# A four-layer transformer block on one core: the order of linear attention, its handover to the expert layer, and the place of three operations in later loops

## Chip, cores and metric

One core of one Trainium2 chip. The metric is device microseconds of one launch, the median of three runs.

## What is computed

The input x is 16 sequences of 256 tokens of 128 features, float32. Four layers follow, each in the same frame:

```
x = x + layernorm(layer(layernorm(x)))
layer 1 (LA):  qkv = u @ W_qkv.T; 16 heads of 8; q = (elu(q)+1)*8**-0.5, k = elu(k)+1
               num, den = causal sums of (q k) v and of q k;  (num / max(den, 1e-6)) @ W_out.T
layer 2 (MOE): s = softmax(u @ centroids.T + biases), the 2 largest of 16 experts weigh Wr[e] u + br[e]
               u + routed + (sum of Ws[e] u + bs[e]) / 2
layer 3 (SA):  layernorm with gain and bias, 16 heads of 64, rotary positions, softmax attention, @ w_out
layer 4 (FFN): gated 128 -> 512 with ternary weights, two 512 -> 512 with gelu, 512 -> 128
```

## The kernel before

Everything stays in SBUF: X holds all 16 sequences (two tiles of 128 tokens each), XnT the normalised transpose that the next layer reads. Each layer is a software pipeline over the 16 sequences: each engine has its own program, a step function called for i = 0 to 15 (the first two or four and the last two written out, the middle in a hardware loop, two steps per turn), and semaphores tie the programs together. The order on each engine is written by hand. An engine runs its instructions in order, so a wait holds back all that stands behind it.

PE (TensorE) does matmuls and transposes, DVE (VectorE) most elementwise work and statistics, ACT (ScalarE) exponentials and copies from PSUM, POOL (GpSimd) the roots of the norms (`rstd_pool`, L363 and L365), the update of X (`residual_pool`, L370), the copy of a sequence's columns into xT (L402), some masks and products.

**Norm.** A norm piece on DVE is statistics (L298), their aggregate (L303), and an application (L314 for the layer's output y, L343 for X), with POOL's root between. Norm 1 has one output norm and one input norm (pieces 0 to 3), norm 2 (after the experts) one output and two input norms (nine fine pieces). PE transposes xn (L383), ACT copies it to XnT (L392).

**Linear attention** (24 to 206.8 us). In step i, PE does scores(i) for two halves (L498), the out product of i-2 (L604), sums(i-1, 1) (L552 for the state, L560), the norm's transposes of i-3 (L383), the v product of i+1 (L454), the turn back (L572), the turn of o (L592), sums(i, 0), the q and k product of i+2 (L443), the state product (L536). DVE: state (L543), divide (L577 to L582), xn (L343), masks (L507), statistics of y (L298), the feature's two halves (L463 "neg", L467), the application (L314). ACT: mask copy (L514), sums copy (L567), XnT copy (L392), v copy (L478, which waits until sums(i-1, 1) is done), exp (L473), blocks (L487). POOL: masks (L520), roots, xT, X, and in each step a part of a check that the last layer's weights are ternary (`ffn_excess_pool`, L1151, L1153, L1155).

**Handover.** After the loop, PE does the router of sequence 0 (L707), one more step, and the norms of sequences 14 and 15; then the first spreads.

**Experts** (238.8 to 437.5 us). For each pair k of experts PE spreads the gates over partitions (`moe_spread_tensor`, L795) into one of four banks, DVE multiplies them with XnT (`moe_scaled_vector`, L804; for pairs 3 and 7, the far ones, ACT copies, L811, and POOL multiplies, L817), and PE multiplies with the expert's weights (L840). "low" (`moe_low_vector`, L783) is the low half of the gates, which the first spread of the next sequence waits for; L714 transposes the gates. DVE's order is the table `MOE_ORDER`.

**Last layer** (1064 us on). `ffn_input_vector` (L1184, L1186) splits XnT of a sequence into high and low parts (fx); PE's products L191 read them; the hidden parts are split by L1191 and L1193 (ff, fh).

## Time and profile before

| | |
|---|---|
| median of 3 runs | 1271.09 us (1270.57 to 1271.78) |
| profiled execution | 1273.35 us, span 1271.5 us, mean granted clock of TensorE 0.976 |
| PE | 1152.8 us busy, 91% of the span |
| DVE | 986.7 us, 78% |
| ACT | 771.9 us, 61% |
| POOL | 568.4 us, 45% |

The stages by their share of the span: linear attention to 206.8 us, handover to 238.8, experts to 437.5, attention to 1020, last layer to the end. Busy shares are means over stages with different limits; the timeline and the waits of a stage tell what ends its steps. In a timeline row the bracket gives how long the engine had been idle and who released it.

### The profile page before, as it was taken

The numbers are of one execution on the slowest core, as the hardware profiler recorded it, in microseconds if no ns is written. First come the engines' busy times: TensorE is split into PE (matmuls) and PEld (weight loads), VectorE is DVE, ScalarE is ACT, GpSimd is POOL, SyncE is SP. The second block draws the span as 40 slices with busy tenths as digits, with TensorE's granted clock in tenths as the row PEclk, the third lists the DMA queues.
The fourth block names the chain that finished last, engine by engine and source line by source line (L and its number), as shares of the span: only waits on it lengthen the run. The fifth ranks groups of instructions, "written<-read, shape, count | busy, mean of one in ns | idle before, by whom it ended". The sixth has DMA issues, their size and how long they took to land.

```text
span 1271.5 us, 32080 instructions
## 1 busy us (share of the span) xinstructions
PE 1152.8 (91%) x10554; PEld 941.7 (74%) x10554; DVE 986.7 (78%) x2499; ACT 771.9 (61%) x2314; POOL 568.4 (45%) x729
## 2 busy tenths in 40 slices
PE   3888886789898869999999999999999997999997
PEld 3555554688888747777777777777777766999997
DVE  6688885588888777778788778787877876788885
ACT  2445553222222249888989888899888894344342
POOL 2777775444444554444545445445444342011112
PEclk9999998799999989999999999999999998999999
DMA  8000000000000000000000000000000000000000
GB/s 282 10 2 0 0 1 2 1 2 1 0 1 0 1 1 2 1 2 1 2 2 1 0 0 0 0 0 0 0 0 0 2 1 1 6 13 12 8 12 19
DMA packets 14303, 12.32 MB, mean 10 GB/s; under 512 B 1778, under 2 KB 12564, under 8 KB 13972
## 3 DMA queue, kind: packets, MB, share of 16 engines
q1 hardware_dynamic: 14228, 11.34, 2.9%
q8 instruction: 44, 0.72, 0.2%
q14 instruction: 31, 0.25, 0.1%
HBM read 9.24 MB, written 2.10 MB: 9 GB/s over the span
## 4 chain that ended last, share of the span: by engine, by line
PE 56%; DVE 14%; issue 8%; POOL 4%; ACT 1%; DVEq 1%; POOLq 0%; ACTq 0%
PE bank L191 14%; PE bank L976 10%; PE bank L1041 10%; PE bank L1070 10%; PE bank L1083 5%; PE bank L840 4%; POOL rstd L365 2%; DVE stat L298 2%; DVE hT L1230 1%; DVE gg L1222 1%; PE bank L795 1%; DVE yn L314 1%; POOL X L370 1%; DVE mv L303 1%; DVE fh_hi L1191 1%
## 5 line engine op out<-in xcount | busy, mean ns | idle before, releaser
L993 ACT ACTIVATE work<-bank,work 128x256 f32<-128x256 f32 x512 | 236.0, 474 | 60.0 <-DVE work L985 59.2
L985 DVE TENSOR_REDUCE work<-bank 128x2 f32<-128x512 f32 x256 | 164.0, 682 | 113.2 <-PE bank L976 113.2
L1007 POOL TENSOR_TENSOR work<-work 128x512 f32<-128x512 f32 x64 | 66.7, 1041 | 279.0 <-DVE work L1001 279.0
L959 POOL TENSOR_TENSOR work<-work 128x512 f32<-128x512 f32 x128 | 164.3, 1284 | 30.2 <-DVE work L951 15.8
L1013 ACT ACTIVATE work<-work 128x256 f32<-128x256 f32 x384 | 161.7, 509 | 0.0
L1041 PE MATMUL bank<-ident,work 128*128 128x128 f32 x1024 | 141.9, 279 | 5.1 <-DVE work L949 1.6
L1041 PEld LDWEIGHTS bank<-ident,work 128*128 128x128 f32 x1024 | 111.7, 141 | 38.5 <-issue 19.9
L1070 PE MATMUL bank<-work 128*64 128x256 f32 x1024 | 138.5, 392 | 0.5 <-DVE work L1056 0.5
L840 PE MATMUL bank<-WrT,moe_work 128*128 128x128 f32 x1024 | 137.4, 278 | 0.7 <-POOL moe_work L817 0.7
L363 POOL TENSOR_SCALAR ve<-mv 128x2 f32<-128x2 f32 x128 | 28.6, 223 | 240.1 <-DVE mv L303 240.1
L976 PE MATMUL bank<-work 32*128 32x256 f32 x2048 | 130.4, 391 | 2.6 <-ACT work L993 1.6
L840 PEld LDWEIGHTS bank<-WrT,moe_work 128*128 128x128 f32 x1024 | 125.4, 192 | 0.9 <-POOL moe_work L817 0.9
L1713 ACT ACTIVATE f<-bank,fs 128x256 f32<-128x256 f32 x128 | 53.8, 472 | 102.3 <-PE bank L191 102.3
L976 PEld LDWEIGHTS bank<-work 32*128 32x128 f32 x2048 | 100.2, 187 | 18.0 <-issue 11.9
L993 ACT ACTIVATION_READ_ACCUMULATOR work<-bank,work 128x1 f32 x512 | 104.4, 204 | 0.0
L1070 PEld LDWEIGHTS bank<-work 128*64 128x64 f32 x1024 | 62.1, 136 | 51.2 <-issue 22.3
L365 POOL TENSOR_TENSOR rstd<-ve,nhalf 128x2 f32<-128x2 f32 x128 | 92.1, 719 | 10.7
L1056 DVE COPY work<-bank 128x512 f32<-128x512 f32 x128 | 81.8, 680 | 6.8 <-PE bank L1041 6.8
L370 POOL TENSOR_TENSOR X<-X,yn 128x256 f32 (+1 forms) x64 | 47.1, 736 | 71.3 <-DVE yn L314 71.3
L191 PE MATMUL bank<-sx_hi,w_lo 128*128 128x256 f32 x256 | 78.8, 308 | 0.0
L795 PE MATMUL bank<-gT,sel 128*128 128x256 f32 x256 | 62.1, 327 | 17.3 <-DVE gT L783 16.8
L1049 ACT ACTIVATE work<-bank 128x512 f32<-128x512 f32 x128 | 69.0, 592 | 10.8 <-PE bank L1041 9.4
(176 smaller groups left out, 2903.9 us busy)
## 6 DMA issues: line engine op xcount, KB each, us to landing
X<-in_x SPq DMA_DIRECT2D x4, 512.0 KB, 5.9
wF<-in_L_ffn_h_w SPq DMA_DIRECT2D x2, 1024.0 KB, 9.7
out<-X SPq DMA_DIRECT2D x16, 128.0 KB, 1.8
w_qkv<-in_L_attn_w_qkv SPq DMA_DIRECT2D x1, 1536.0 KB, 9.2
WrT<-in_L_ffn_Wr SPq DMA_DIRECT2D x1, 1024.0 KB, 5.1
w_out<-in_L_attn_w_out SPq DMA_DIRECT2D x1, 512.0 KB, 10.5
wF<-in_L_ffn_w_w SPq DMA_DIRECT2D x2, 256.0 KB, 8.5
rope_sin<-in_rope_sin SPq DMA_DIRECT2D x1, 256.0 KB, 3.2
```

Of the source, the lines that this page charges most:

```text
L191: ins = nc.tensor.matmul(out, x_, y_, start=start and k == 0, stop=stop and k == len(products) - 1)
L365: nc.gpsimd.tensor_tensor(rstd[:, :], ve[:, :], nhalf[:, 0:T], ALU.pow).then_inc(n_rstd[r], 1)
L795: ins = nc.tensor.matmul(XB[k % 4][:, e * LEN:(e + 1) * LEN], sel[:, 2 * k + e, :], gT[:, p, :], start=True, stop=True)
L840: ins = nc.tensor.matmul(moe_y(p)[:, t, :], x_, WrT[:, (2 * k + e) * E:(2 * k + e + 1) * E], start=False, stop=(k == XPAIRS - 1 and e == 1 ...
L959: nc.gpsimd.tensor_tensor((QT if kind == "q" else KT)[:, p, a, :], rc[:, ru % 2, :], rs_[:, ru % 2, :], ALU.add).then_inc(c_rope, 1)
L976: ins = nc.tensor.matmul(SB_[j][:, t * LEN:(t + 1) * LEN], QT[rows, p, a, s * LEN + t * P:s * LEN + (t + 1) * P], KT[rows, p, a, s * LEN:( ...
L985: nc.vector.tensor_reduce(nmax[:, QUAD * a + j, :], SB_[j][:, :].rearrange("p (t k) -> p t k", t=T), AX.X, ALU.max, negate=True).then_inc( ...
L993: ins = nc.scalar.activation(pr[:, a % 2, j, t, :], SB_[j][:, t * LEN:(t + 1) * LEN], ACT.Exp, bias=nmax[:, h, t:t + 1], accum_out=psum_[: ...
L1013: ins = nc.scalar.activation(pr[:, a % 2, j, t, :], pr[:, a % 2, j, t, :], ACT.Copy, scale=prec[:, h, t:t + 1])
L1041: ins = nc.tensor.transpose(TURN_BANKS[j][:, kt * LEN + t * P:kt * LEN + (t + 1) * P], pr[:, a % 2, j, t, kt * P:(kt + 1) * P], ident[:, :])
L1056: nc.vector.tensor_copy(pT[:, j, :, :], TURN_BANKS[j][:, :].rearrange("p (t q) -> p t q", t=T))\
L1070: ins = nc.tensor.matmul(OB[e * D:(e + 1) * D, k * LEN:(k + 1) * LEN], V[:, p, kt, h * D:(h + 1) * D], pT[:, 2 * k + e, kt, :], start=(kt ...
```

## The change

Linear attention: on PE, the v product comes first after the scores, the norm's transposes wait for the v copy, and out stands behind them; the state product comes ahead of the turn back. DVE does the feature's halves earlier, ACT exp, v copy and blocks earlier. The router of sequence 0 goes into step 15, its copy of columns into step 14. The steps after the loop are written out anew: sequence 15's norm goes into step 0 of the experts, the last two checks behind POOL's first two expert steps, and the banks of the spreads are in another order. Experts: in `MOE_ORDER` "low" stands ahead of norm piece 3 and "next 0" ahead of piece 5; on POOL the far product of pair 7 stands ahead of the first input root. Last layer: the input is split two sequences ahead, between two norm pieces. The diff, with unchanged lines thinned out and indentation cut; the sum Wsh moves unchanged from behind the loop into steps 2 and 3, and the waits of PE for a_m, a_me, a_o and n_yn after the loop are removed:

```diff
@@ -396,8 +396,9 @@
...
-if l == MOE and i_is(i, 0, 1):
-    pool.wait_ge(a_v, SEQS)
+if l == MOE:
+    if i_is(i, 0, 1):
+        pool.wait_ge(a_v, SEQS - 1 + i)
     pool.wait_ge(n_xnT[1], i + 1)
 nc.gpsimd.tensor_copy(xT[:, p, :], seq_cols(XnT, i)).then_inc(x_ready[l], 1)
@@ -449,7 +450,6 @@
 pe.wait_ge(x_ready[LA], i + 1)
 pe.wait_ge(a_va, reached(i))
 pe.wait_ge(a_state, reached(i - 1))
-pe.wait_ge(n_xnT[1], reached(i - 3))
@@ -681,7 +681,7 @@
...
-RB, XB, YB_M = bank[1], bank[2:6], bank[6:8]
+RB, XB, YB_M = bank[1], (bank[4], bank[5], bank[3], bank[2]), bank[6:8]
@@ -842,8 +842,9 @@
...
+MOE_LAST_NORM = (1, 2, 5, 7)
 MOE_ORDER = (("norm", 0), ("norm", 1), ("pair", 4), ("late", 4), ("late", 5), ("late", 6), ("late", 7), ("pair", 5),
-         ("norm", 2), ("pair", 6), ("norm", 3), ("norm", 4), ("low", 0), ("norm", 5), ("next", 0),
+         ("norm", 2), ("pair", 6), ("low", 0), ("norm", 3), ("norm", 4), ("next", 0), ("norm", 5),
          ("early", 0), ("norm", 6), ("norm", 7), ("early", 1), ("next", 1), ("early", 2), ("norm", 8),
          ("early", 3), ("next", 2))
@@ -1325,7 +1326,9 @@
...
-    if not i_is(i, SEQS - 2, SEQS - 1):
+    if i_is(i, SEQS - 2, SEQS - 1):
+        pool_xT(pool, MOE, i - (SEQS - 2), p)
+    else:
         pool_xT(pool, LA, i + 2, p)
...
     if not i_is(i, 0, 1):
         norm_pool(pool, 1, i - LA_LAG, 1)
+    if not i_is(i, 0, 1, SEQS - 1):
         ffn_excess_pool(pool, i - LA_LAG, p)
 over_sequences(pool, la_step, 4)
-pool_xT(pool, MOE, 0, 0)
-pool_xT(pool, MOE, 1, 1)
-for i in range(SEQS - LA_LAG, SEQS):
-    for k in range(ROUNDS[1]):
-        norm_pool(pool, 1, i, k)
-for i in range(SEQS - LA_LAG, SEQS):
-    ffn_excess_pool(pool, i, i % 2)
-pool.wait_ge(n_xnT[1], SEQS)
+rstd_pool(pool, 1, SEQS - 2, 0)
+residual_pool(pool, 1, SEQS - 2)
+rstd_pool(pool, 1, SEQS - 2, 1)
+ffn_excess_pool(pool, SEQS - 3, 1)
 moe_far_pool(pool, 0, FAR)
 def moe_step(i, p):
-    lag = not i_is(i, 0)
-    if lag:
-        rstd_pool(pool, 2, i - 1, 0)
+    r, of = (1, SEQS - 1) if i_is(i, 0) else (2, i - 1)
+    rstd_pool(pool, r, of, 0)
     if not i_is(i, SEQS - 2, SEQS - 1):
         pool_xT(pool, MOE, i + 2, p)
-    if lag:
-        residual_pool(pool, 2, i - 1)
-        rstd_pool(pool, 2, i - 1, 1)
+    residual_pool(pool, r, of)
     moe_far_pool(pool, i, 4 + FAR)
-    if lag:
-        rstd_pool(pool, 2, i - 1, 2)
+    rstd_pool(pool, r, of, 1)
+    if r == 2:
+        rstd_pool(pool, r, of, 2)
     if not i_is(i, SEQS - 1):
         moe_far_pool(pool, i + 1, FAR)
+    if i_is(i, 0, 1):
+        ffn_excess_pool(pool, SEQS - 2 + i, p)
 over_sequences(pool, moe_step)
@@ -1458,6 +1458,8 @@
...
+    if more:
+        la_feat_vector(dve, i + 1, 1 - p, 0)
     if not i_is(i, 0):
         la_state_vector(dve, i - 1)
         la_divide_vector(dve, i - 1, 0)
@@ -1466,21 +1468,27 @@
     if live:
         for g in range(1, LA_GROUPS):
             la_mask_vector(dve, i, 0, g)
+    if more:
+        la_feat_vector(dve, i + 1, 1 - p, 1)
     if not i_is(i, 0, 1):
         run_piece(1, n1, 0, i - LA_LAG, p)
-    if more:
-        la_feat_vector(dve, i + 1, 1 - p, 0)
     if not i_is(i, 0):
         la_divide_vector(dve, i - 1, 1)
     if not i_is(i, 0, 1):
         run_piece(1, n1, 1, i - LA_LAG, p)
-    if more:
-        la_feat_vector(dve, i + 1, 1 - p, 1)
     if live:
         for g in range(1, LA_GROUPS):
             la_mask_vector(dve, i, 1, g)
     if not i_is(i, 0, 1):
         run_piece(1, n1, 2, i - LA_LAG, p)
+    if i_is(i, 2):
...
+        nc.vector.tensor_tensor(Wsh[:, :], WsT[:, 0, :], WsT[:, 1, :], ALU.add).then_inc(s_wsh, 1)
+    if i_is(i, 3):
...
+        nc.vector.scalar_tensor_tensor(Wsh[:, :], Wsh[:, :], 0.5, ident[:, :], ALU.mult, ALU.add)\
+            .then_inc(s_wsh, 1)
 over_sequences(dve, la_step, 4)
@@ -1489,22 +1497,21 @@
...
 for part in range(MOE_EXP_PART):
     moe_router_vector(dve, rch, 0, 0, part)
...
-la_step(SEQS, 0)
-run_piece(1, n1, 3, SEQS - 2, 0)
+la_state_vector(dve, SEQS - 1)
+la_divide_vector(dve, SEQS - 1, 0)
+run_piece(1, n1, 3, SEQS - 3, 1)
 for part in range(MOE_EXP_PART, MOE_ROUTER_PARTS):
     moe_router_vector(dve, rch, 0, 0, part)
 rch.end()
-for k in range(len(n1)):
-    run_piece(1, n1, k, SEQS - 1, 1)
+run_piece(1, n1, 0, SEQS - 2, 0)
+la_divide_vector(dve, SEQS - 1, 1)
+run_piece(1, n1, 1, SEQS - 2, 0)
 moe_low_vector(dve, 0, 0)
-for k in range(FAR):
-    moe_scaled_vector(dve, 0, k)
+moe_scaled_vector(dve, 0, 0)
+moe_scaled_vector(dve, 0, 1)
+run_piece(1, n1, 2, SEQS - 2, 0)
+moe_scaled_vector(dve, 0, 2)
+run_piece(1, n1, 3, SEQS - 2, 0)
@@ -1512,8 +1519,13 @@
 def moe_step(i, p):
     for what, part in MOE_ORDER:
-        if what == "norm" and not i_is(i, 0):
-            run_piece(2, n2, part, i - 1, 1 - p)
+        if what == "norm":
+            if not i_is(i, 0):
+                if i_is(i, 1) and part == len(n2) - 1:
+                    dve.wait_ge(n_tp[1], SEQS)
+                run_piece(2, n2, part, i - 1, 1 - p)
+            elif part in MOE_LAST_NORM:
+                run_piece(1, n1, MOE_LAST_NORM.index(part), SEQS - 1, 1)
@@ -1590,8 +1602,8 @@
...
-    if more:
-        ffn_input_vector(dve, i + 1)
+    if i_is(i, 0):
+        ffn_input_vector(dve, 1)
     for m in range(2):
@@ -1605,6 +1617,9 @@
     if behind:
         ffn_out_vector(dve, i - 1, 1 - p)
         run_piece(4, n4, 0, i - 1, 1 - p)
+    if not i_is(i, SEQS - 2, SEQS - 1):
+        ffn_input_vector(dve, i + 2)
+    if behind:
         run_piece(4, n4, 1, i - 1, 1 - p)
 over_sequences(dve, ffn_step)
@@ -1624,45 +1639,47 @@
...
+    if more:
+        la_exp_scalar(act, i + 1)
     if live:
         la_mask_scalar(act, i, 0)
+    if more:
+        la_v_scalar(act, i + 1, 1 - p)
     if not i_is(i, 0):
         la_sums_scalar(act, i - 1, 1)
     if not i_is(i, 0, 1, 2):
         norm_scalar(act, 1, i - LA_TURN_LAG, TB[:, 0:LEN])
     if more:
-        la_v_scalar(act, i + 1, 1 - p)
-        la_exp_scalar(act, i + 1)
+        la_blocks_scalar(act, i + 1, 1 - p)
     if live:
         la_mask_scalar(act, i, 1)
     if not i_is(i, 0):
         la_turn_scalar(act, i - 1)
-    if more:
-        la_blocks_scalar(act, i + 1, 1 - p)
     if live:
+        la_ktok_scalar(act, i)
         la_sums_scalar(act, i, 0)
-        la_ktok_scalar(act, i)
     if not i_is(i, 0, 1, 2):
         ffn_excess_scalar(act, i - LA_LAG - 1, 1 - p)
 over_sequences(act, la_step, 4)
 moe_router_scalar(act, 0, 0)
-la_step(SEQS, 0)
+la_sums_scalar(act, SEQS - 1, 1)
+norm_scalar(act, 1, SEQS - 3, TB[:, 0:LEN])
+moe_gates_scalar(act, 0, 0)
+la_turn_scalar(act, SEQS - 1)
 norm_scalar(act, 1, SEQS - 2, TB[:, 0:LEN])
-moe_gates_scalar(act, 0, 0)
-norm_scalar(act, 1, SEQS - 1, TB[:, 0:LEN])
...
-for i in range(SEQS - 2, SEQS):
-    ffn_excess_scalar(act, i, i % 2)
...
     if not i_is(i, 0, 1):
         norm_scalar(act, 2, i - 2)
+    if i_is(i, 1):
+        norm_scalar(act, 1, SEQS - 1)
     if more:
...
     if more:
         moe_far_scalar(act, i + 1, FAR)
+    if i_is(i, 0, 1, 2):
+        ffn_excess_scalar(act, SEQS - 3 + i, 1 - p)
@@ -1744,52 +1763,55 @@
...
     if live:
         la_scores_tensor(pe, i, p, 0)
-    if not i_is(i, 0, 1):
-        la_out_tensor(pe, i - 2)
+    if more:
+        la_v_tensor(pe, i + 1, 1 - p)
     if not i_is(i, 0):
         la_sums_tensor(pe, i - 1, 1 - p, 1)
     if not i_is(i, 0, 1, 2):
+        pe.wait_ge(a_va, at_most_all(i + 2))
         pe.wait_ge(a_state, i)
         norm_tensor(pe, 1, i - LA_TURN_LAG, TB)
-    if more:
-        la_v_tensor(pe, i + 1, 1 - p)
+    if not i_is(i, 0, 1):
+        la_out_tensor(pe, i - 2)
     if not i_is(i, 0):
         la_back_tensor(pe, i - 1, 1)
     if live:
         la_scores_tensor(pe, i, p, 1)
-    if i_is(i, SEQS - 1, SEQS):
-        pe.wait_ge(n_xnT[1], i - LA_TURN_LAG + 1)
+    if i_is(i, SEQS - 1):
+        pe.wait_ge(s_w[MOE], 16 * 4)
+        pe.wait_ge(a_feat, SEQS)
+        moe_router_tensor(pe, 0, 0)
     if not i_is(i, 0):
+        pe.wait_ge(n_xnT[1], reached(i - LA_TURN_LAG + 1))
         la_turn_tensor(pe, i - 1)
     if live:
         la_sums_tensor(pe, i, p, 0)
+        la_ktok_tensor(pe, i, p)
     if not i_is(i, SEQS - 2, SEQS - 1, SEQS):
         la_qk_tensor(pe, i + 2, p)
     if live:
-        la_ktok_tensor(pe, i, p)
+        la_state_tensor(pe, i, p)
         la_back_tensor(pe, i, 0)
-        la_state_tensor(pe, i, p)
 over_sequences(pe, la_step, 4)
...
-moe_router_tensor(pe, 0, 0)
-la_step(SEQS, 0)
-la_out_tensor(pe, SEQS - 1)
-norm_tensor(pe, 1, SEQS - 2, TB)
+la_sums_tensor(pe, SEQS - 1, 1, 1)
+pe.wait_ge(a_state, SEQS)
+norm_tensor(pe, 1, SEQS - 3, TB)
+la_out_tensor(pe, SEQS - 2)
+la_back_tensor(pe, SEQS - 1, 1)
 moe_gates_tensor(pe, 0, 0)
-norm_tensor(pe, 1, SEQS - 1, TB)
...
+pe.wait_ge(n_xnT[1], SEQS - 2)
+la_turn_tensor(pe, SEQS - 1)
...
-for k in range(4):
+for k in range(FAR):
     moe_spread_tensor(pe, 0, 0, k)
+la_out_tensor(pe, SEQS - 1)
+norm_tensor(pe, 1, SEQS - 2, TB)
+pe.wait_ge(n_xnT[1], SEQS - 1)
+moe_spread_tensor(pe, 0, 0, FAR)
 moe_router_tensor(pe, 1, 1)
...
             moe_spread_tensor(pe, i, p, k + 4)
         elif more:
             moe_spread_tensor(pe, i + 1, 1 - p, k - 4)
+        if k == 0 and i_is(i, 1):
+            norm_tensor(pe, 1, SEQS - 1)
         if k == 0 and not i_is(i, 0, 1):
+            if i_is(i, 2):
+                pe.wait_ge(n_xnT[1], SEQS)
             norm_tensor(pe, 2, i - 2)
         if k == 2 and more:
             moe_gates_tensor(pe, i + 1, 1 - p)
```

## Rows read from the trace of the kernel before

**Rows 1.** Busy time by stage: start:end, us, then each engine, clock, DMA share, GB/s.

```profile
75.66:206.80 131.14, 113.71 (x1372) 76.24 (x1370) 109.58 (x322) 70.11 (x175) 93.77 (x130) 1.00 0.00 1
206.80:238.80 32.00, 14.78 (x87) 11.53 (x87) 13.88 (x59) 4.52 (x15) 15.13 (x24) 0.60 0.00 1
238.80:437.50 198.70, 177.47 (x1510) 172.01 (x1510) 162.72 (x585) 47.75 (x155) 93.25 (x154) 1.00 0.00 1
```

**Rows 2.** Timeline of one linear attention step: start us, us, engine, line, operation.

```profile
108.86 0.41 PE L536 MATMUL bank<-la_work 128*128 128x144 f32 x2
...
110.28 0.71 PE L604 MATMUL bank<-la_out,la_work 128*128 128x128 f32 x4
...
110.83 1.06 PE L552 MATMUL bank<-la_work 128*128 128x128 f32 x8
...
112.96 0.60 ACT L567 ACTIVATE la_work<-bank 128x512 f32<-128x512 f32 x1 [2.00 <-PE bank L560]
...
113.98 0.68 PE L454 MATMUL bank<-la_qkv,xT 128*128 128x128 f32 x4 [0.71 <-ACT XnT L392]
...
114.70 0.38 ACT L478 ACTIVATE la_work<-bank 128x256 f32<-128x256 f32 x1 [0.86 <-PE bank L454]
...
117.07 1.88 DVE L507 TENSOR_TENSOR la_work<-bank,tri 128x512 f32<-128x512 f32 x3
...
119.93 0.42 PE L536 MATMUL bank<-la_work 128*128 128x144 f32 x2
```

**Rows 3.** Timeline between the stages, 206 to 240 us.

```profile
211.28 1.00 PE L707 MATMUL bank<-centT,xT 128*128 128x16 f32 x4 [4.39 <-POOL xT L402]
...
215.71 2.08 PE L552 MATMUL bank<-la_work 128*128 128x128 f32 x8 [2.39 <-DVE la_work L582]
...
226.04 0.69 PE L383 MATMUL bank<-ident,xn 128*128 128x128 f32 x2 [2.34 <-DVE xn L343]
...
233.41 0.69 PE L383 MATMUL bank<-ident,xn 128*128 128x128 f32 x2 [5.89 <-DVE xn L343]
...
238.90 1.80 PE L840 MATMUL bank<-WrT,moe_work 128*128 128x128 f32 x8
```

**Rows 4.** Timeline of one expert step, all engines.

```profile
344.04 0.49 DVE L298 BATCH_NORM_STATS2 stat<-X 128x6 f32 x2 [0.50 <-POOL X L370]
...
344.91 0.42 DVE L783 TENSOR_TENSOR gT<-bank,gT 32x256 fp32r<-32x256 f32 x1
...
345.46 0.50 PE L795 MATMUL bank<-gT,sel 128*128 128x256 f32 x2 [1.28 <-DVE gT L783]
...
346.05 1.09 POOL L817 TENSOR_TENSOR moe_work<-moe_work,XnT 128x512 f32<-128x512 f32 x1
346.11 1.37 DVE L343 TENSOR_SCALAR xa<-X,mv,rstd 128x128 f32 x2 [0.78 <-POOL rstd L365]
```

**Rows 5.** What PE waited for in 262 to 430 us: total, times, longest.

```profile
PE bank L795 <- DVE gT L783: 16.1, 13, 1.3
```

**Rows 6.** Timeline of PE, gate transposes of expert steps 1 and 14.

```profile
253.61 0.38 PE L714 MATMUL bank<-ident,moe_work 128*128 128x128 f32 x2
...
417.01 0.41 PE L714 MATMUL bank<-ident,moe_work 128*128 128x128 f32 x2
```

**Rows 7.** Timeline of DVE and POOL in two neighbouring linear attention steps.

```profile
110.24 0.63 DVE L343 TENSOR_SCALAR xn<-X,mv,rstd 128x128 f32 x2
...
121.50 1.17 DVE L343 TENSOR_SCALAR xn<-X,mv,rstd 128x128 f32 x2
...
121.73 0.86 POOL L1153 TENSOR_TENSOR cube<-cube,wF 128x320 f32<-128x320 f32 x1
```

**Rows 8.** Timeline of one step of the last layer.

```profile
1160.95 0.38 PE L191 MATMUL bank<-fx_lo,w_hi 128*128 128x256 f32 x1 [0.20 <-DVE fx_lo L1186]
...
1161.80 0.42 DVE L1191 CAST ff_hi<-f 128x512 fp32r<-128x512 f32 x1
...
1167.64 0.69 DVE L1193 TENSOR_TENSOR fh_lo<-hT,fh_hi 128x512 fp32r<-128x512 f32 x1
```

15 lines of the change are left out of this document (3 added, 12 removed).

## The prediction

> **What bounds the kernel now.** I read the busy times by stage first [rows 1], then one step of each loop in order of time, then what each wait ends on. The attention layer (437.5 to 1020 us) is untouched and is not argued about. In linear attention DVE is busy 109.6 of 131.1 us and PE 113.7, and neither is full: the step is a ring of latencies. It takes 11.06 us (the state product starts at 108.86 and 119.93) [rows 2]. Its old ring: divide, sums (L552), the copy of the sums 2.13 us later (112.96), the copy of XnT, and only then the v product, whose wait is put down to ACT L392, then the turn back and the second divide. In the 32 us between the stages PE is busy 14.8 us at a granted clock of 0.60 [rows 1]: latency alone. The reader is to see there that the router of sequence 0 stands first in PE's queue and sits 4.39 us for POOL's copy, that the last sequence's sums (L552) wait behind it until 215.71, and that the transposes of sequences 14 and 15 come at 226.04 and 233.41, each at the end of a whole norm [rows 3]. In the expert loop PE is the busiest (177.5 of 198.7 us), but it stops once a step for 1.28 us for the low gates (L795 waits for DVE L783) [rows 4], in all 13 times, 16.1 us [rows 5]. A step takes (417.01 - 253.61) / 13 = 12.57 us [rows 6].
>
> **Expert loop.** In DVE's order "low" moves ahead of the statistics of X, where DVE waits 0.50 us for POOL anyway; its 0.42 us fit in. Put at the wait's beginning (344.04 less 0.50) it ends at 343.96, and PE, which is done with the previous product 1.28 us before 345.46, at 344.18, no longer waits: 12.57 - 1.28 = 11.3 us is then PE's own time [rows 4]. DVE must follow. The scaled product "next 0" (its DVE group spacing is 0.6 us, 0.69 long) moves from behind the first normalisation into the 0.78 us that L343 waits for the root: gain 0.60, given that the earlier spread has filled its bank, which the first point gives. POOL's far product (1.09 us, L817) moves ahead of the root. Today it starts at 346.05, and L343, two instructions of DVE, start at 346.11 and take 1.37 us [rows 4]; free of POOL such a pair takes 0.63 us, and where POOL's L1153 starts 0.23 us after its start it takes 1.17 [rows 7]. With the far product over before the root, L343 falls to 0.6: gain 0.77. What it costs: the statistics end at about 344.9, and the far product, started behind the update of X at 344.0 to 344.1, ends at 345.2, so the root starts 0.2 us later: loss 0.2. DVE: 0.60 + 0.77 - 0.2 = 1.17 us a step, to 11.4 us; PE's 11.3 lies just below. Take 11.4 to 11.45: 1.14 x 14 steps = 16 us. Bounds: 0.4 a step (6 us) if the overlap only moves to another pair of instructions, 1.28 (18 us) if PE alone decides. The three weight checks (POOL, 2.5 us each by the same lines as L1153) that used to stand in the tail now end POOL's first expert steps; behind them is queued the root of the next sequence, about 1 us late in two steps, partly covered by PE's own work: -1 us (0 to -2). Expert loop: 15.
>
> The Trainium skill, "SBUF — State Buffer", section "Who interferes with whom", says the pair of ports shared by DVE and GpSimd is an exclusive lock and that who issues first decides who blocks. The rows on L343 agree (0.63 against 1.17 and 1.37). It also says a DVE instruction with two SBUF inputs contends with GpSimd's reads, which speaks against the move in the last layer: by it the split of the input (L1186) and the root would take turns, and the sum there would lose 0.4 us a step of slack that it has.
>
> **Linear attention loop (11 steps of it are steady).** Same instructions, another order: exp and the v product come early, out comes behind the norm's transposes, and "neg" stands first on DVE. I count DVE's own work as (109.6 + 1.3 for what the last step lacks) / 12 = 9.25 us, 9.35 with gaps between instructions [rows 1], and add the waits of the new order. (a) PE's transposes now wait for the v copy (a_va), and that copy waits until the sums of the previous sequence have left va. From L552: 2.13 us to ACT [rows 2], 0.38 the v copy, 0.06 to PE, 0.35 the transposes, 0.71 + 0.04 the out product: 3.67 us until the statistics of y can start. DVE has in that time xn 0.55, three masks 1.8, the feature 0.65: 3.0, so it waits about 0.7 to 0.8. The added wait has out, the turn back and scores queued behind it on PE, and DVE's statistics wait for out. (b) Statistics to root to L314: 2.07 us, as 344.04 to 346.11 in the expert step [rows 4]; DVE has in it the statistics 0.84 and a divide 0.70: waits 0.5. Step: 9.35 + 0.75 + 0.5 = 10.6, say 10.65, against 11.06: 0.41 x 11 = 4.5 us. PE has 113.7 / 12 = 9.5 us of work in it, POOL 93.8 / 12 = 7.8 [rows 1]; neither is the bound. Bounds: with L343 and the check's L1153 colliding in every step (now at 1.17 in every second one, where DVE's waits still absorb it [rows 7]) 0.55 more, 11.2 us, -1.5 in all; without (a) 9.9 us, +13, of which I keep 9 for the range. The first four steps are held up by POOL's weight split; 1 us from the earlier masks (0 to 2). The weight sum Wsh (0.6 us of DVE) moves into steps 2 and 3, where DVE idles for POOL: nothing; without that cover 0.6.
>
> **Between the stages.** The router of sequence 0 goes inside step 15, its copy is made in step 14, and POOL's checks no longer stand before it. From the loop's end to L552 it was 215.71 - 206.8 = 8.9 us [rows 1, 3]. New: DVE still has the last statistics, half the router and one divide to do (an estimate of 3.5 us by the same instructions in this tail), and PE idles that long. Gain 5.4. Then the norm of sequence 15 leaves the chain: 226.04 to 233.41 is its two roots, 7.4 us [rows 3], of which about 0.8 stays as instructions between the spreads: gain 6.6. The spreads of pairs 0 to 2 go to banks 4, 5 and 3 and start before sequence 14 is normalised; pair 3 (bank 2) waits for its transposes, so sequence 14's second root is late next. So from the loop's end to the first pair product 20 us, against 238.90 - 206.8 = 32.1. Gain 12; bounds 7 (PE at half clock throughout, and step 0 of the experts held up by sequence 15's norm) and 14. That norm lies in step 0, where DVE has no norm of its own and PE's 10.4 us of products cover it; uncovered it costs 3.
>
> **Last layer.** The split of the input (fx) two sequences ahead frees PE from the stall at 1160.95 (0.36 us with pipeline). But the next product waits for fh_lo, which ends at 1167.64 + 0.69 = 1168.33, just as PE arrives [rows 8]. Its chain runs on DVE from the split of gelu's second half (L1191, 1161.80), and that waits for gelu, so with the input split out of the way it starts only about 0.12 us earlier. 0.12 x 14 = 1.5 us; bounds 0 and 0.36 x 13 = 4.5. The root covers the moved split; without that cover it costs as before.
>
> **Sum.** 15 + 4.5 + 1 + 12 + 1.5 = 34 us. The profiled execution took 1273.35 us (span 1271.5); 1273.35 - 34 = 1239.4. The median of the runs shown is 1271.09, 2.3 us lower, so 1237 to 1239: **1239**.
>
> **Rivals.** *The far product only changes its victim*: "low" frees PE, but DVE keeps 12.1 us a step (the 0.77 is not gained). For: POOL and DVE still touch SBUF together; against: in the new place DVE reads PSUM or runs statistics. 34 - 10 = 24: 1247 us. *The v copy closes a worse ring in linear attention*: a and b longer and L343 hit in each step, 11.2 us or up to 11.5. For: the copy stands in ACT's queue between the sums and their own copy; against: only 0.3 us of it is new. 34 - 6 to -10: 1247. *Both loops keep their periods*, another wait taking the place of each one removed, and only the tail gains: 1271.1 - 12 - 2 = 1257. *The change does not act*: waits are only renamed, because the old ones were satisfied late by something else: 1271; against it stands the 4.39 us that POOL's queue alone causes. *Slower*: TensorE's granted clock. Before the tail it is 1.00, in the tail 0.60 [rows 1], and there L552 takes 2.08 us, against 1.06 at full clock [rows 3, 2]. If the gathered waits of the new loop let the clock fall to its lower level, PE's 9.5 us a step become some 17: +6 a step, +72 in twelve; it decides as soon as it holds in five of the twelve steps (5 x 6 = 30). Against: PE idles less a step in total than now.
>
> **How the numbers follow.** Forecast (1228 to 1246) 0.54; far product 0.17; worse ring 0.12; tail only 0.08; no action 0.04; slower 0.05. Range: below, all upper bounds but one, 1226; above, to the tail-only case, 1258. What lies outside is the slower case, no action, and the ends of the others. 0.2% is 2.5 us, about what this kernel's measurement tells from no change. Faster 0.91, within 0.2% 0.04, slower 0.05.
>
> **What would show it.** After: no wait of L795 for L783; xa's L343 pair at 0.6 us; gates transposes (L714's group) every 11.4 us; state products every 10.65 us with PE's transposes waiting for the v copy and DVE's statistics for out; the first pair product some 20 us after the last state product; fx gone from PE's waits and fh_lo in its place. Wrong: expert steps above 12 us, linear attention steps above 11, or a granted clock under 0.9 in either loop.

## The result and the profile after

The changed kernel takes **1242.28 us** (median of 4 runs, 1240.65 to 1242.91), the kernel before beside it 1271.43 (4 runs, 1270.57 to 1272.84): a ratio of 0.9768, 95% interval 0.9751 to 0.9785. It is 29 us faster; 34 were forecast. The profiled execution has a span of 1239.9 us, against 1271.5.

Busy time by stage, as in [rows 1] (us, then PE, PEld, DVE, ACT and POOL busy, granted clock): linear attention's steps from 3 on, the stretch to the first pair product, and the experts. The fourth line is the stretch ahead of the last layer.

```profile
73.04:201.80 128.76, 111.87 (x1373) 77.57 (x1372) 110.64 (x323) 69.44 (x175) 94.68 (x133) 1.00 0.00 1
201.80:223.10 21.30, 12.05 (x86) 9.97 (x87) 12.06 (x53) 4.81 (x17) 8.07 (x12) 0.76 0.00 1
223.10:409.80 186.70, 178.16 (x1512) 173.00 (x1512) 155.39 (x593) 48.13 (x158) 100.40 (x164) 0.99 0.00 1
...
1020.00:1067.00 47.00, 36.95 (x288) 33.21 (x287) 32.36 (x80) 21.52 (x59) 6.79 (x12) 0.96 0.01 2
```

In the experts PE does the same work as in [rows 1] with 12.7 us less idle time (186.70 - 178.16 against 198.70 - 177.47). Between the stages PE works 12.05 us instead of 14.78, at a granted clock of 0.76 instead of 0.60 (the router of sequence 0, four matmuls, and the transposes of one norm are no longer in this stretch, and four matmuls of the turn back are now), and its idle time falls from 17.2 to 9.3 us. The same points in both traces give the ledger (start of each point, us):

| from | to | before | after | gain | forecast |
|---|---|---|---|---|---|
| 0 | first state product (L536) | 41.10 | 39.60 | 1.5 | 0 |
| first | last state product | 165.37 | 162.20 | 3.2 | 5.5 |
| last state product | first pair product (L840) | 32.43 | 21.30 | 11.1 | 12 |
| first pair product | first attention product (L191) | 198.62 | 186.65 | 12.0 | 15 |
| that | first yf of the last layer | 659.7 | 657.7 | 2.0 | 0 |
| first yf | last yf | 167.9 | 166.1 | 1.8 | 1.5 |

**The experts.** PE's gate transposes of expert steps 3 and 14, and DVE and POOL in one step between them, which answers to [rows 4] and [rows 6]:

```profile
265.04 0.44 PE L714 MATMUL bank<-ident,moe_work 128*128 128x128 f32 x2
...
324.08 0.42 DVE L783 TENSOR_TENSOR gT<-bank,gT 32x256 fp32r<-32x256 f32 x1
324.55 0.49 DVE L298 BATCH_NORM_STATS2 stat<-X 128x6 f32 x2
...
324.77 1.09 POOL L817 TENSOR_TENSOR moe_work<-moe_work,XnT 128x512 f32<-128x512 f32 x1 [0.38 <-PE bank L840]
325.83 0.22 POOL L363 TENSOR_SCALAR ve<-mv 128x2 f32<-128x2 f32 x1
...
326.89 0.60 DVE L343 TENSOR_SCALAR xa<-X,mv,rstd 128x128 f32 x2 [0.65 <-POOL rstd L365]
...
390.33 0.44 PE L714 MATMUL bank<-ident,moe_work 128*128 128x128 f32 x2
```

(390.33 - 265.04) / 11 = 11.39 us a step, before 12.57. The low gates (L783) stand ahead of the statistics, L795 waits for them no more, the far product runs beside DVE's statistics and a product from PSUM, and L343's pair takes 0.60 us instead of 1.37. The root is what DVE still waits for.

**The first steps of the experts** are not as good: the gate transposes stand at 228.12, 239.66, 253.37 and 265.04, so that one distance is 13.71 us. There POOL does a check of the weights (three instructions, L1152 to L1156) ahead of the root:

```profile
250.50 0.72 POOL L1152 TENSOR_TENSOR cube<-wF 128x320 f32<-128x320 f32 x1
251.37 0.86 POOL L1154 TENSOR_TENSOR cube<-cube,wF 128x320 f32<-128x320 f32 x1
...
251.41 0.83 DVE L750 TENSOR_TENSOR moe_work<-moe_work 128x4 f32<-128x4 f32 x1
...
252.37 0.86 POOL L1156 TENSOR_TENSOR cube<-cube,wF 128x320 f32<-128x320 f32 x1
...
252.54 0.77 DVE L761 TENSOR_TENSOR moe_work<-moe_work 128x64 f32<-128x64 f32 x1
...
253.20 0.22 POOL L363 TENSOR_SCALAR ve<-mv 128x2 f32<-128x2 f32 x1
...
254.25 0.73 DVE L314 TENSOR_SCALAR yn<-bank,mv,rstd 128x128 f32<-128x128 f32 x2 [0.34 <-POOL rstd L365]
```

The check delays the root, and two small instructions of DVE that read SBUF twice take 0.83 and 0.77 us beside it; in a step without a check the same ones take 0.16 and 0.23 (at 332.77 and 333.25 us).

**Linear attention and the stretch behind it.** What the engines waited for in ten steps (84.1 to 195 us: total, times, longest), and PE's timeline behind the loop, which answers to [rows 3]:

```profile
PE bank L454 <- DVE la_work L543: 6.4, 10, 1.0
PE bank L383 <- ACT la_work L478: 6.3, 10, 0.7
...
DVE yn L314 <- POOL rstd L365: 5.4, 10, 0.5
...
DVE stat L298 <- PE bank L604: 4.9, 10, 0.7
```

```profile
201.80 0.52 PE L536 MATMUL bank<-la_work 128*128 128x144 f32 x2 [0.37 <-ACT la_work L532]
...
205.89 2.07 PE L552 MATMUL bank<-la_work 128*128 128x128 f32 x8 [2.94 <-DVE la_work L582]
...
218.90 0.69 PE L383 MATMUL bank<-ident,xn 128*128 128x128 f32 x2 [3.51 <-DVE xn L343]
...
223.10 2.02 PE L840 MATMUL bank<-WrT,moe_work 128*128 128x128 f32 x8
```

The state products stand alternately 10.59 and 11.20 us apart, mean 10.9 (before 11.06). Behind the loop the router is gone, L552 begins 4.1 us after the last state product, and only one norm stands ahead of the first pair product.

**A point on reading totals.** Each kernel has one trace, and the first state product moves from one to the next: 39.60 us here, 37.8 and 37.9 in two experiments (a_place, a_router), in each of which the change from this kernel lies much later. PE's first products show where it begins, in the changed kernel and in the run a_place:

```profile
25.97 1.22 PE L444 MATMUL bank<-xT,la_qkv 128*128 128x256 f32 x2 [1.18 <-ACT XnT L659]
```

```profile
25.43 0.70 PE L444 MATMUL bank<-xT,la_qkv 128*128 128x256 f32 x2 [1.17 <-ACT XnT L659]
```

The same two products take 1.22 us in the one and 0.70 in the other, which I read as TensorE's slower and faster level; nothing in what tells these two kernels apart comes before it. Their F differ by 1.8 us, 0.5 of it already there when these products start. So below all distances count from the first state product, F.

The 1.5 us between the kernel before and the changed one are of another kind. There the first products take 1.22 us in both, and PE is within 0.1 us of the same time up to 38.5 us. Then the order tells, before and after:

```profile
40.61 0.66 PE L572 MATMUL bank<-ident,la_work 128*128 128x128 f32 x4 [0.89 <-ACT la_work L567]
```

```profile
39.60 0.41 PE L536 MATMUL bank<-la_work 128*128 128x144 f32 x2
```

Before, the state product stood behind the turn back, which waits 0.89 us for ACT; now it stands ahead of it. The scores that follow both start 0.9 us earlier (40.53 instead of 41.45), so of the 1.5 us 0.9 are gained, and in some 0.6 only the point F has moved within its step.

### The profile page after: what moved, and what is told of

The parts are those of the page before. It is cut to its first block, busy times and chain, and to the rows that moved or that the text cites. A ratio compares the mean times of both kernels' runs of the same rounds, so it can differ in the third digit from the quotient of the medians.

```text
span 1239.9 us, 32078 instructions
## 1 busy us (share of the span) xinstructions
PE 1142.7 (92%) x10554; PEld 937.9 (76%) x10554; DVE 979.5 (79%) x2499; ACT 768.2 (62%) x2314; POOL 570.4 (46%) x729
## 4 chain that ended last, share of the span: by engine, by line
PE 72%; DVE 11%; issue 7%; POOL 5%; ACT 2%; DVEq 1%; POOLq 0%; ACTq 0%
PE bank L191 23%; PE bank L977 10%; PE bank L1042 10%; PE bank L1071 10%; PE bank L1084 5%; PE bank L840 4%; PE bank L1258 2%; POOL rstd L365 2%; DVE la_work L507 2%; DVE stat L298 2%; PE bank L560 1%; PE bank L552 1%; PE bank L795 1%; PE bank L383 1%; DVE mv L303 1%
## 5 line engine op out<-in xcount | busy, mean ns | idle before, releaser
L960 POOL TENSOR_TENSOR work<-work 128x512 f32<-128x512 f32 x128 | 164.2, 1283 | 29.6 <-DVE work L952 15.6
L840 PE MATMUL bank<-WrT,moe_work 128*128 128x128 f32 x1024 | 137.9, 279 | 0.0
L840 PEld LDWEIGHTS bank<-WrT,moe_work 128*128 128x128 f32 x1024 | 126.0, 193 | 0.0
L191 PE MATMUL bank<-sx_hi,w_lo 128*128 128x256 f32 x256 | 78.7, 307 | 0.0
L191 PE MATMUL bank<-sx_lo,w_hi 128*128 128x256 f32 x256 | 72.5, 283 | 0.0
```

Source lines behind the costliest of these rows:

```text
L191: ins = nc.tensor.matmul(out, x_, y_, start=start and k == 0, stop=stop and k == len(products) - 1)
L840: ins = nc.tensor.matmul(moe_y(p)[:, t, :], x_, WrT[:, (2 * k + e) * E:(2 * k + e + 1) * E], start=False, stop=(k == XPAIRS - 1 and e == 1 ...
L960: nc.gpsimd.tensor_tensor((QT if kind == "q" else KT)[:, p, a, :], rc[:, ru % 2, :], rs_[:, ru % 2, :], ALU.add).then_inc(c_rope, 1)
```

## The experiments

F to the last state product, from there to the first pair product, from there to the first yf, and the 15 steps of the last layer (all us; F itself ahead). The time is a median of four runs for before, after, a_oldloop, a_checks, a_place and a_split, of ten for e_ffn, and a single run for the others; the kernel before, run again beside the experiments, had medians of 1271.47 to 1273.29 and single runs from 1269.42 to 1275.95, so a total of one run tells no difference of 2 or 3 us, and the stretches carry the argument.

| kernel | F | F to last state | to pair product | to first yf | last layer | time |
|---|---|---|---|---|---|---|
| before | 41.10 | 165.37 | 32.43 | 858.3 | 167.9 | 1271.43 |
| e_order | 41.19 | 164.86 | 32.56 | 850.0 | 168.1 | 1264.98 |
| e_far | 40.98 | 164.76 | 32.14 | 855.4 | 167.8 | 1269.26 |
| e_both | 41.36 | 165.36 | 32.44 | 843.0 | 168.0 | 1258.31 |
| e_ffn | 40.14 | 164.80 | 32.52 | 856.7 | 165.3 | 1269.72 |
| e_loop | 41.26 | 161.68 | 34.65 | 858.8 | 167.3 | 1271.79 |
| after | 39.60 | 162.20 | 21.30 | 844.4 | 166.1 | 1242.28 |
| a_oldloop | 40.81 | 165.92 | 19.70 | 844.3 | 165.3 | 1244.28 |
| a_router | 37.87 | 169.84 | 20.74 | 844.9 | 165.7 | 1247.23 |
| a_vlate | 39.40 | 166.75 | 21.52 | 844.5 | 165.9 | 1246.21 |
| a_far | 39.39 | 162.31 | 21.31 | 854.0 | 165.6 | 1250.75 |
| a_checks | 39.61 | 162.27 | 22.79 | 841.7 | 166.1 | 1240.48 |
| a_place | 37.79 | 162.28 | 20.87 | 844.6 | 165.7 | 1239.69 |
| a_split | 39.37 | 165.54 | 22.28 | 846.2 | 165.5 | 1245.84 |

### The experts' two halves: e_order, e_far, e_both

The kernel before with DVE's new order alone:

```diff
-                     ("norm", 2), ("pair", 6), ("norm", 3), ("norm", 4), ("low", 0), ("norm", 5), ("next", 0),
+                     ("norm", 2), ("pair", 6), ("low", 0), ("norm", 3), ("norm", 4), ("next", 0), ("norm", 5),
```

> The kernel before with DVE's table of the expert step alone changed (low ahead of the statistics of X, next 0 ahead of the first input norm); POOL's order stays. My theory (the 0.60 us of next 0 and the 0.77 us of the overlap are two separate gains): the far product still starts with the root's end, so L343 on xa stays at 1.37 us; the wait of L795 for L783 (16.1 us in 13 times) goes; the step falls by about 0.6 us from 12.57 to 12.0. Rival (the low gates alone were the price): PE is free, so the step falls by the whole 1.28 us, to 11.3.

with POOL's far product ahead of the root alone:

```diff
+                moe_far_pool(pool, i, 4 + FAR)
                 if lag:
                     residual_pool(pool, 2, i - 1)
                     rstd_pool(pool, 2, i - 1, 1)
-                moe_far_pool(pool, i, 4 + FAR)
```

(the product stands between the update of X and the root), and with both:

> The kernel before with POOL's far product moved ahead of the first input root, nothing else. My theory (DVE's L343 is held by POOL's L817, and DVE's own sum sets the step): L343 on xa falls from 1.37 to 0.6 us and the step by 0.77 - 0.2 = about 0.55 us, to 12.0, although L795 still waits for L783. Rival (the wait for the low gates sets the step, and the norm's time is hidden): no change, 12.57. Rival 2: the far product holds another DVE instruction in its new place, no change.

> The kernel before with both edits of the expert step and nothing else. My theory: the two gains add, step 11.4 us, 15 to 16 us off the time of the kernel before. Rival: they overlap, 11.8 to 12.0.

Measured, by the gate transposes of expert steps 1 and 14 as in [rows 6]: 11.89 us with the order (-0.68), 12.25 with the far product (-0.32), 11.40 with both (-1.17, more than the sum). The tile xa of the run with the order, of the run with the far product and of both (min/median/max ns of one instruction):

```profile
L343 DVE TENSOR_SCALAR xa<-X,mv,rstd x32: 332/724/1283, 257.7 to 441.3; 128x128 f32 x24, 128x128 f32<-128x128 f32 x8
```

```profile
L343 DVE TENSOR_SCALAR xa<-X,mv,rstd x32: 335/345/1282, 258.4 to 445.8; 128x128 f32 x24, 128x128 f32<-128x128 f32 x8
```

```profile
L343 DVE TENSOR_SCALAR xa<-X,mv,rstd x32: 335/344/1283, 258.3 to 434.4; 128x128 f32 x24, 128x128 f32<-128x128 f32 x8
```

Each half acts as the steps of the prediction say: only the far product's place shortens L343, only the order takes PE's wait for the low gates away. In e_far that wait stays and DVE stands longer for the root:

```profile
DVE xa L343 <- POOL rstd L365: 12.8, 11, 1.4
PE bank L795 <- DVE gT L783: 12.5, 11, 1.3
```

So more than half of the 0.77 us that the far product's place saves on L343 runs into waits as long as the order is old, and the step gains 0.32 us where about 0.55 were expected. With both, the step is the one expected, and from the first pair product to the first yf 15.3 us are gained; the single run's total is 13.1 us under 1271.43.

### The far product back, in the changed kernel: a_far

```diff
                 residual_pool(pool, r, of)
-                moe_far_pool(pool, i, 4 + FAR)
                 rstd_pool(pool, r, of, 1)
+                moe_far_pool(pool, i, 4 + FAR)
```

> The changed kernel with GpSimd's far product put back behind the root in the expert layer, all else left. Theory: VectorE's statistics step (the two scalar operation of line 343) falls under GpSimd's far product again, 722 instead of 344 ns (median), and VectorE's wait for the root goes from 0.8 us to about 0.4; the step grows from 11.39 to 11.7 to 11.9 us, over 14 steps 4 to 7 us: 1247 to 1249 us. It is the change alone on top of the other half, where before alone on the kernel before it gave 0.32 us a step and the order alone 0.68, both 1.17. Rival (the far product matters only as it delays the root, not by what shares the memory with it): the step stays at 11.5 or below, under 2 us.

```profile
319.48 1.37 DVE L343 TENSOR_SCALAR xa<-X,mv,rstd 128x128 f32 x2 [0.36 <-POOL rstd L365]
```

The pair takes 1.37 us again, the wait for the root falls to 0.36, the step is (398.23 - 267.30) / 11 = 11.90 us. The loss is 9.6 us from the pair product to the first yf, more than the 4 to 7 expected: 0.51 us in each of the 11 later steps and 0.75 in each of the first three make 7.9 of it, and the rest lies behind the loop. The far product's place is worth 0.51 where the order is new and 0.32 where it is old. The sum in the prediction (0.60 + 0.77 - 0.20 = 1.17) is met to the hundredth, but that is in part luck: of its two parts the order gave 0.68 instead of 0.60, and the far product behind it 0.49 instead of 0.57, and they are not additive.

### The checks: a_checks and a_place

a_checks moves the checks of sequences 13 and 14 right behind the loop, where POOL is idle, and that of 15 ahead of the first far product (ACT's halves likewise):

```diff
+            ffn_excess_pool(pool, SEQS - 3, 1)
+            ffn_excess_pool(pool, SEQS - 2, 0)
             rstd_pool(pool, 1, SEQS - 2, 0)
             residual_pool(pool, 1, SEQS - 2)
             rstd_pool(pool, 1, SEQS - 2, 1)
-            ffn_excess_pool(pool, SEQS - 3, 1)
+            ffn_excess_pool(pool, SEQS - 1, 1)
...
-                if i_is(i, 0, 1):
-                    ffn_excess_pool(pool, SEQS - 2 + i, p)
```

> The changed kernel with the checks of the last three sequences taken out of the first expert steps on GpSimd and ScalarE: those of sequences 13 and 14 go directly behind the loop, where GpSimd was idle for 7 us, that of 15 into the stretch ahead of the first pair product. Theory: the checks in expert steps 0 and 1 (2.7 us of GpSimd each) held back the root, and with it VectorE, by some 2.4 us in all beside what they did to VectorE's small operations; without them the steps 1 and 2 take about 11.4 us each instead of 11.5 and 13.7, and the first pair product stands within 0.5 us of 223.1 us: 1.5 to 3.5 us less in all, ratio to the changed kernel 0.997 to 0.999. Rival A (steps 1 and 2 are long because the norm of the last sequence of linear attention is run in them as well): within 0.7 us. Rival B (the checks in the handover hold back the root of sequence 14's norm): first pair product 1.5 us or more later and no gain.

The first steps take 10.80, 11.44 and 11.49 us instead of 11.54, 13.71 and 11.67: 3.2 us, so the checks are what held them, and rival A falls. But the first pair product stands at 224.67 and the first gate transposes 2.2 us later, so the first half of rival B holds too (the root of sequence 14 is held back), but not its second, since a gain is left. The trace shows how it starts (DVE, 204 to 208 us):

```profile
204.63 0.70 DVE L743 TENSOR_TENSOR moe_work<-iota,moe_work 128x64 f32<-128x64 f32 x1
...
206.16 1.18 DVE L343 TENSOR_SCALAR xn<-X,mv,rstd 128x128 f32<-128x128 f32 x2
```

L743 takes 0.70 instead of 0.23 us and L343 1.18 instead of 0.59. L552 begins 0.4 us later, and the rest grows behind it: four matmuls of the out product take 1.06 us instead of 0.61. Windows of 4 us from 206 and 210 us show a granted clock of 0.50 and 0.72, in the changed kernel 0.58 and 1.00. Net, the first yf comes 1.1 us earlier, and the time is 1240.48 us, ratio to the kernel before 0.9751 (0.9731 to 0.9771); the intervals of this and of the changed kernel overlap.

a_place puts the checks of sequences 13 and 14 where DVE does nothing; that of sequence 15 goes into step 0, step 1 has none, and ACT's halves follow. On POOL behind the loop:

```diff
+            pool.wait_ge(b_g, 1)
+            ffn_excess_pool(pool, SEQS - 3, 1)
             rstd_pool(pool, 1, SEQS - 2, 0)
             residual_pool(pool, 1, SEQS - 2)
             rstd_pool(pool, 1, SEQS - 2, 1)
-            ffn_excess_pool(pool, SEQS - 3, 1)
+            pool.wait_ge(n_xn[1], SEQS - 1)
+            ffn_excess_pool(pool, SEQS - 2, 0)
```

> The changed kernel with the checks of the last three sequences placed otherwise on GpSimd than in the run that moved all three ahead of the first pair product, which made that product 1.57 us later and gained 3.2 us behind it. Here the one of sequence 13 starts only when VectorE has done its last small gate product (207.14 us in the changed kernel; VectorE is then idle to 210.50 us), the one of 14 only when VectorE's line 343 for sequence 14 is done, and the one of 15 stands in the first expert step. Theory (a check costs when it runs beside VectorE's short operations or delays the root, and nothing in VectorE's idle time): the first pair product is not later than 223.1 us (0.4 to 1 us earlier, since line 343 takes 0.60 instead of 0.99 us), one expert step is longer than 11.4 us by 1 to 1.5 us and the rest are not: 2 to 3 us in all, 1239.3 to 1240.3 us. Rival (what makes the first product late is TensorE's granted clock, which any shift of its work here lowers): the first product at 224 us or later, total within 1 us of the changed kernel.

```profile
205.48 0.72 POOL L1152 TENSOR_TENSOR cube<-wF 128x320 f32<-128x320 f32 x1 [2.75 <-DVE moe_work L761]
...
216.07 0.60 DVE L343 TENSOR_SCALAR xn<-X,mv,rstd 128x128 f32<-128x128 f32 x2 [0.61 <-POOL rstd L365]
...
220.94 2.02 PE L840 MATMUL bank<-WrT,moe_work 128*128 128x128 f32 x8
...
223.18 1.91 PE L840 MATMUL bank<-WrT,moe_work 128*128 128x128 f32 x8
```

L343 takes 0.60 us and the first pair product comes 0.43 us earlier after the last state product; the one long step takes 12.73 us instead of 13.71. But the second pair product takes 1.91 us, not 1.57: PE is at its slower level for longer, and the first gate transposes stand 26.30 us behind the last state product, in the changed kernel 26.32. Of the 1.2 us gained in the steps 0.3 is left at the first yf (865.4 us behind the last state product, against 865.7); at the attention layer's first product it is still 1.1, and 0.9 is given back from there to the first yf, where nothing was changed and where the runs differ by up to 3.3 us among themselves (657.4 to 660.7 us). The median, 1239.69 us (ratio 0.9749, 0.9725 to 0.9773), is the lowest of all, but its own trace owes 1.8 us of its 2.4 to F. So neither placing is shown to beat the changed kernel: what they free in the steps is 1 to 3 us, and in these traces TensorE's lower level or the next wait takes most of it.

### The loop of linear attention: e_loop, a_oldloop

e_loop is the kernel before with the new order of the loop's steps on DVE, ACT and PE; a_oldloop is the changed kernel with the old one. For PE the edit is (and the reverse in a_oldloop):

```diff
-                if not i_is(i, 0, 1):
-                    la_out_tensor(pe, i - 2)
+                if more:
+                    la_v_tensor(pe, i + 1, 1 - p)
...
-                if more:
-                    la_v_tensor(pe, i + 1, 1 - p)
+                if not i_is(i, 0, 1):
+                    la_out_tensor(pe, i - 2)
```

> The kernel before with only the new order of linear attention's loop on VectorE, ScalarE and TensorE (and without the wait that kept the v product behind the transposed norm); GpSimd's order, the handover and the experts as before. Theory: the changed kernel's linear attention steps of 10.59 and 11.20 us in turns (mean 10.9, before 11.06) come from this order alone, so here too: 2.5 us less over the loop's even stretch and some 2.5 us less in the first three steps. The handover from the loop's end to the first pair product stays near 32 us (before) and the expert steps stay at 12.57 us. Total 4 to 6 us under the kernel before. Rival (the handover's 11 us were in part the loop's, since the new order leaves less behind at the loop's end): total 8 us or more under, with a handover of 28 us or less. Second rival (the loop gains only because GpSimd's last checks and copies left it): total within 1.5 us of the kernel before.

> The changed kernel with the old order of linear attention's loop on VectorE, ScalarE and TensorE (with the old wait of the v product), all else left: GpSimd's early copies, the new handover, the experts. On the kernel before the new order alone made TensorE's last state product 3.5 us earlier and the total did not move, because the router behind the loop stood for GpSimd. Theory (in the changed kernel the router no longer stands for GpSimd, so the loop's time goes through): the even steps take 11.06 us again, the last state product stands 3 to 4 us later after the first one than in the changed kernel (162.2 us between them), the handover from there to the first pair product stays at 21.3 us within 0.7, total 3 to 4.5 us over the changed kernel: 1245.3 to 1246.8 us. Rival (the old order leaves less to be done behind the loop, or the new handover has room of its own): the handover shrinks by 2 us or more and the total stays within 1 us of the changed kernel.

e_loop has the changed kernel's steps (10.60 and 11.20 us in turns) and leaves the loop 3.7 us sooner after F, and the total does not move: 1271.79 us. The theory's total falls, and the second rival's number comes without its reason, since the steps themselves do gain; the time is lost at once. PE behind the loop:

```profile
202.94 0.52 PE L535 MATMUL bank<-la_work 128*128 128x144 f32 x2 [0.37 <-ACT la_work L531]
...
209.24 1.00 PE L706 MATMUL bank<-centT,xT 128*128 128x16 f32 x4 [5.16 <-POOL xT L402]
...
237.59 2.02 PE L839 MATMUL bank<-WrT,moe_work 128*128 128x128 f32 x8
239.25 0.78 PE L794 MATMUL bank<-gT,sel 128*128 128x256 f32 x2
239.82 1.84 PE L839 MATMUL bank<-WrT,moe_work 128*128 128x128 f32 x8
```

The router waits 5.16 us for POOL's copy, against 4.39 in [rows 3]; of 3.5 us at the last state product 2.0 are left at the router, 1.3 at the first pair product, and 0.2 at the first gate transposes, since the second pair product takes 1.84 us at the slower level where before it took 1.06. In a_oldloop the steps are 11.06 us again and the last state product 3.7 us later, as the theory has it, but the handover shrinks to 19.70 us, by 1.6, so neither the theory (within 0.7) nor the rival (2 or more) has it whole; 2.1 us of the 3.7 go through, and the time is 1244.28 us (ratio 0.9777, 0.9761 to 0.9794), under the 1245.3 that was expected at least. From F to the first pair product it takes 197.8 us before, 185.6 with the new handover alone and 183.5 in the changed kernel. So the loop's new order alone leaves the total where it was (196.3 us over this stretch, of which the experts' first products lose most), and is worth about 2 us with the new handover, while the handover alone is worth 12.2, and both together 14.3.

### The early copy and router: a_router

```diff
-                if i_is(i, SEQS - 2, SEQS - 1):
-                    pool_xT(pool, MOE, i - (SEQS - 2), p)
-                else:
+                if not i_is(i, SEQS - 2, SEQS - 1):
                     pool_xT(pool, LA, i + 2, p)
...
+            pool_xT(pool, MOE, 0, 0)
+            pool_xT(pool, MOE, 1, 1)
             rstd_pool(pool, 1, SEQS - 2, 0)
```

> The changed kernel with GpSimd's two copies of the experts' input put back behind linear attention's loop; TensorE's router for the first sequence stays inside the last step, ahead of the turn, and waits for the copy there. In the run with only the loop's new order on the kernel before, TensorE left the loop 3.5 us earlier and the total did not move: its router waited 5.16 us for this copy. Theory (in the old handover VectorE and TensorE stood for that copy, and its move is a large part of the handover's gain of 11 us): the first router product falls from inside the last step to 205 us or later, TensorE waits 3 to 5 us for it, VectorE's selection and then everything to the first pair product follow: 223.1 becomes 226 to 228.5 us, total 3 to 5.5 us over the changed kernel. Rival (the handover's gain lies in the order of norm, gates and spread behind the loop): the first pair product within 1 us of 223.1.

```profile
203.56 1.00 PE L707 MATMUL bank<-centT,xT 128*128 128x16 f32 x4 [5.70 <-POOL xT L403]
```

PE stands 5.70 us for the copy inside the last step and then works at half clock (granted 0.50 from 202 to 214 us). From F to the first pair product it takes 190.6 us against 183.5: 7.1 us, more than the 3 to 5.5 expected. The absolute numbers, 228.45 us for the first pair product and 1247.23 for the kernel, lie in the expected ranges only because F comes 1.7 us earlier in this trace. The theory holds; the wait itself is 5.70 us, and how much of the rest the lower clock makes was not tried apart.

### What sets linear attention's step: a_vlate, a_split

a_vlate exchanges ACT's copy of v and its copy of the earlier sums:

```diff
-                if more:
-                    la_v_scalar(act, i + 1, 1 - p)
                 if not i_is(i, 0):
                     la_sums_scalar(act, i - 1, 1)
+                if more:
+                    la_v_scalar(act, i + 1, 1 - p)
```

> The changed kernel with one exchange on ScalarE in linear attention: the copy of the sums of the sequence before goes ahead of the copy of v. In the changed kernel TensorE's state product waits 0.73 and 0.56 us a step for the copy of v and VectorE's exponent step 0.28 and 0.65 us for TensorE. Theory (this ring through the copy of v sets the step): the copy of v lands about 0.5 us later, and each step grows by 0.4 to 0.7 us, 5 to 9 us over 14 steps: 1247 to 1251 us. Rival (the step is set by the DVE work and the copy of the sums is what somebody waits for): the step shrinks or stays, within 1.5 us of the changed kernel. The expert steps stay at 11.39 us in both.

The copy of v starts 0.44 us later, PE's wait for it goes from 6.3 to 10.6 us in the ten steps, DVE's for the out product from 4.9 to 9.2, and each step grows by 0.43 us (11.02 and 11.64 in turns): 1246.21 us. The waits of a_vlate in the same stretch:

```profile
PE bank L383 <- ACT la_work L478: 10.6, 10, 1.2
...
DVE stat L298 <- PE bank L604: 9.2, 10, 1.1
```

The 0.44 us put into this ring show in the step whole, so the ring through the copy of v is the bound, and it is the one that the prediction named (a). The step is as expected; the total, 1246.21 us, is just under the expected 1247 to 1251, since only some ten steps grow and not 14.

a_split takes POOL's check away from under L343, by putting two of its products behind the mask's first half and the third behind the copy of xT:

```diff
+                if not i_is(i, 0, 1, SEQS - 1):
+                    ffn_excess_pool(pool, i - LA_LAG, p, (0, 1))
...
+                if not i_is(i, 0, 1, SEQS - 1):
+                    ffn_excess_pool(pool, i - LA_LAG, p, (2,))
...
-                if not i_is(i, 0, 1, SEQS - 1):
-                    ffn_excess_pool(pool, i - LA_LAG, p)
```

> The changed kernel with GpSimd's check of a sequence's weights split in linear attention's steps: its first two products go ahead of GpSimd's product with the mask's first half, the third behind the copy of xT, instead of all three at the step's end, where VectorE's statistics step (line 343) runs beside them for 1.20 us in every second step and 0.76 in the others, against 0.60 beside nothing. Theory (the two lengths of step, 10.59 and 11.20 us, come from this meeting of line 343 with the check): line 343 takes about 0.6 us in all steps, every step takes 10.4 to 10.8 us, and 11 steps give 1.5 to 4 us: 1238.5 to 1241 us. Rival (the two lengths come from the ring through TensorE, ScalarE's copy of v and VectorE's exponent step, and line 343 only moves waiting about): the steps keep their mean within 0.1 us, no gain. Second rival (the two products, now ahead of the mask's product, make VectorE or TensorE wait for that): a loss of 2 us or more.

DVE, one step of the changed kernel and one of a_split, both of the longer kind:

```profile
141.57 1.23 DVE L343 TENSOR_SCALAR xn<-X,mv,rstd 128x128 f32 x2
...
145.43 0.49 DVE L298 BATCH_NORM_STATS2 stat<-bank 128x6 f32<-128x128 f32 x2 [0.24 <-PE bank L604]
```

```profile
144.28 0.60 DVE L343 TENSOR_SCALAR xn<-X,mv,rstd 128x128 f32 x2
...
148.15 0.49 DVE L298 BATCH_NORM_STATS2 stat<-bank 128x6 f32<-128x128 f32 x2 [0.82 <-PE bank L604]
```

L343 takes 0.60 us in every step, and the steps stay at 10.60 and 11.20: the 0.6 us saved turn into a longer wait for the out product. The theory falls and the first rival holds. The second and third distance between state products grow by 1.7 and 1.3 us (12.39 and 14.27), the handover by 1.0, and the time is 1245.84 us (ratio 0.9786, 0.9758 to 0.9814); the second rival's loss of 2 us is there too, but the causes of it were not tried apart.

The traces show where the 0.6 us between the two kinds of step enters. In the changed kernel, in the longer step:

```profile
139.96 0.69 DVE L463 TENSOR_SCALAR la_work<-bank 128x512 f32<-128x512 f32 x1 [0.40 <-issue]
```

```profile
141.20 0.60 PE L454 MATMUL bank<-la_qkv,xT 128*128 128x128 f32 x4 [0.98 <-DVE la_work L543]
```

DVE stands 0.40 to 0.43 us ahead of L463 for nothing that the profile shows ("issue"), at 96.39, 118.18, 139.96 and 161.74 us, and these are the four steps of 11.20 us. L543 and the v product behind it come later by it: L454 waits 0.98 us for L543, in the shorter step 0.41, and starts 2.96 us behind the state product instead of 2.33. That is ahead of the copy of v, in the ring. The four gaps stand in a_split as well. They come once per turn of the hardware loop, and L463 is now the first instruction of DVE's step; in the old order that was L543, which waits 0.68 to 0.79 us for PE in each step anyway. So the turn of the loop is the likely cause, but no run moves it, and that part is not shown.

### The last layer: e_ffn

```diff
-                if more:
-                    ffn_input_vector(dve, i + 1)
+                if i_is(i, 0):
+                    ffn_input_vector(dve, 1)
...
+                if not i_is(i, SEQS - 2, SEQS - 1):
+                    ffn_input_vector(dve, i + 2)
```

> The kernel before with the last layer's input split moved and nothing else. My theory (fh_lo is next late right behind fx_lo): the step shortens by 0.12 us of the 0.36 us stall, 1.8 us in all, and a wait for fh_lo appears. Rival: the whole stall is gained, 0.36 x 13 = 4.7 us. Rival from the lock that the Trainium skill states (SBUF - State Buffer, Who interferes with whom): the split takes turns with the root, the update of X comes later, nothing gained.

The steps take (1259.46 - 1094.13) / 15 = 11.02 us, before 11.19, so 2.6 us over the layer, more than the 1.8 expected and less than the rival's 4.7; ratio 0.9976 (0.9963 to 0.9990) over 10 runs. The rest of its span lies ahead of the layer. PE's wait for fx_lo is gone from the steps, and the wait for fh_lo is there, as the theory has it: PE and its weight loads wait for fh_lo 12 times, before 2. What the theory overlooked is the split's own length. In its old place its second instruction, L1186, ran beside POOL's update of X and took 0.85 us (median of 16; 1.00 at 1159.82 us); in the new one it takes 0.43, while the root beside it takes 0.87. Another instruction now meets the update of X:

```profile
1132.89 1.11 DVE L1193 TENSOR_TENSOR ff_lo<-f,ff_hi 128x512 fp32r<-128x512 f32 x1
1134.28 0.43 DVE L1191 CAST ff_hi<-f 128x512 fp32r<-128x512 f32 x1 [0.28 <-ACT f L1716]
1134.74 0.69 DVE L1193 TENSOR_TENSOR ff_lo<-f,ff_hi 128x512 fp32r<-128x512 f32 x1
```

The first ff_lo takes 1.11 us and the second 0.69: POOL's update of X (1132.70 us) runs beside the first. It costs nothing, since DVE then still waits 0.28 us for gelu.

## Why the prediction was right, step by step

**Expert step.** Forecast 11.4 to 11.45, measured 11.39; the wait for the low gates gone, L343 at 0.60, the root next in line, all as written. The Trainium skill's rule on the shared ports ("SBUF — State Buffer", "Who interferes with whom") agrees with a_far, where the pair goes from 0.60 to 1.37 us by POOL's order alone.

**The checks in the first steps** were mis-sized: 1 us was taken off (0 to 2), and a_checks gives 3.2 us back in the first steps when they leave. The term counted only the delay of the root, less what PE's work covers; the trace shows beside it 0.67 and 0.54 us on two small instructions of DVE. That is 2.2 of the 3 us by which the experts' 12 fall short of 15; another 0.9 lie between the first pair product and the first gate transposes (5.02 us, before 4.13), where the second pair product takes 1.57 us instead of 1.06.

**Linear attention's loop.** Ring (a) was the right one (a_vlate), and its waits are there: 0.73 and 0.56 us for v's copy, 0.24 to 0.28 and 0.65 at the out product, 0.54 for the root. The step was put at 10.65, the shorter kind is 10.59, and every second one is 0.6 longer, which is above the 11 us that was to be a sign of being wrong; the mean, 10.9, is not. This is the term that was mis-sized: the steps were to give 4.5 us, and from the first to the last state product there are 3.2, the first steps' share included. The sum had nothing for two kinds of step; the bound that it gave, L343 under the check, is excluded by a_split, and the traces show 0.40 us ahead of L463 in every second step instead, which goes through the ring. Further, the terms were added as if the loop's gain passed through: e_loop shows that it doesn't pass the old handover, and a_oldloop that 2.1 of 3.7 us pass the new one.

**Between the stages.** 20 us were forecast and 21.3 measured. From the loop's end to L552 the forecast had 3.5 us, measured 4.1; one norm is gone from the chain; sequence 14's second root is late next, as said: L383 waits 3.51 us for it and L343 takes 0.99 beside the check. Taking the early copies out costs 7.1 us (a_router); what they would give with the router left behind the loop was not run.

**Last layer.** 0.12 us a step forecast, 0.12 measured in the changed kernel and 0.17 in e_ffn, and fh_lo is next late, as written. The same rule of the Trainium skill ("SBUF — State Buffer", "Who interferes with whom") was read on the wrong pair of instructions: the split kept its 0.43 us beside the root, whose 128x2 grew from 0.71 to 0.87, and the 0.4 us fell on ff_lo, which has two SBUF inputs as the rule says, beside the update of X. Before, the same rule had acted on the split itself: L1186 took 0.85 us beside that update, which the prediction did not count.

**What was luck.** 2.0 of the 31.6 us between the spans lie between the attention layer's first product and the first yf, where nothing was changed: over the last 47 us ahead of the first yf the granted clock is 0.96 against 0.85 before, and in the runs the stretch takes 657.4 to 660.7 us whatever was changed. Without it the traces gain 29.6 us on what the change touches, against the forecast's 34; the medians gain 29.15. The 1.5 us ahead of F had no term in the sum; with them linear attention and the handover gain 15.8 us where 17.5 were forecast. And the time, 1239 forecast and 1242.28 measured, is closer than the gain, because the 34 us were taken from a profiled execution that was 2.3 us slower than its median. The rival that ended slower, a lower clock in linear attention, did not come: 1.00 in that loop.

## What to carry to other kernels

Ask of a gain ahead of a handover what the next stage's first instruction waits for; if it is another engine's queue, the gain ends there, and both have to be moved together. Put a background task not where its own engine is idle, but where the engine that shares the memory with it is; even then a stretch in which TensorE mostly waits can take the gain back by its clock. And before a single trace's total is read as a gain of 1 or 2 us, line the traces up at the first product of the first loop, one that stands at the same place in both orders.

## What the runs showed of the hardware

- Small instructions of DVE suffer most for their size: a tensor_tensor of 128x4 that reads SBUF twice takes 0.83 us instead of 0.16 beside POOL's check, one of 128x64 0.77 instead of 0.23; POOL's own instructions there take 0.86.
- At the start of a kernel the same matmuls took 1.22 us in one trace and 0.70 in another (at 25 us; F lies 1.8 us apart), as at the two levels of TensorE's clock, while the clock column of the 20 to 30 us window read 1.00 in both traces. The Trainium skill ("TensorE: Matmul & The Clock Gate", "What's actually happening") says that how many first matmuls run slow differs from run to run of one kernel; these rows agree.
- The moment at which the clock rose behind a stretch of single waits differed with what stood in it: the second pair product, the same eight matmuls, took 1.57 us in the changed kernel, 1.91 in a_place, 1.84 in e_loop and 1.06 in the kernel before.
